# Expert tokens by quarter-row gathers and VectorE block transposes, and three reorderings around the last tile and the choice of tokens

## What is computed

```
x = x + xattn(layernorm(x), ctx)          # attention without softmax over 128 keys
x = x + fp6_ffn(layernorm(x))             # operands quantised in blocks of 32, dequantised, multiplied
x = x + mix(layernorm(x), ctx)            # x @ W1.T + a mean of ctx @ W2.T + b
x = x + moe(layernorm(x))

logits = x @ Wg + bg;  probs = softmax(logits over the tokens)      # 16 experts
vals, idx = top_k(probs per batch and expert, 128)
tok = x[idx]                                                        # 128 tokens of 512
h = relu(tok @ w1 + b1); h = relu(h @ w2 + b2); h = h @ w3 + b3     # per expert, 512x512 each
out[idx] += h * vals
```

## Time and profile before

| | |
|---|---|
| median of 3 runs | 740.56 us (740.15 to 741.81) |
| the profiled execution | 738.98 us |
| its span in the trace | 737.2 us |
| busy, share of the span | PE 97%, DVE 71%, ACT 55%, POOL 57% |
| DMA | 118 MB, mean 160 GB/s |
| mean granted TensorE clock | 0.99 of full |

### The profile page before, as it was taken

How to read it: one execution, slowest core, us unless ns; L and a number is a source line. 1 busy time by engine, 2 the same in 40 slices (tenths; PEclk the granted TensorE clock), 3 DMA queues, 4 the chain that set the end, 5 groups by cost and what they waited for, 6 DMA issues and landing times.

```text
span 737.2 us, 12752 instructions
## 1 busy us (share of the span) xinstructions
PE 714.1 (97%) x4506; PEld 623.2 (85%) x4506; DVE 520.4 (71%) x978; ACT 402.0 (55%) x680; POOL 421.6 (57%) x621
## 2 busy tenths in 40 slices
PE   6999999999999999999999899999999999999995
PEld 5765888888888888888888878798999899899894
DVE  5785789889888898875897798463664556363561
ACT  5755444454554445868668533454664556464641
POOL 2825789888888887876878722604430442340132
PEclk9999999999999999999999999999999999999998
DMA  8710122222212213110116998796895798995544
GB/s 311 267 30 15 44 73 76 76 85 73 89 60 87 86 58 103 44 61 29 61 60 242 334 401 296 191 366 186 234 372 165 192 355 268 298 274 157 143 86 58
DMA packets 61671, 118.04 MB, mean 160 GB/s; under 512 B 6056, under 2 KB 7464, under 8 KB 61608
## 3 DMA queue, kind: packets, MB, share of 16 engines
q1 hardware_dynamic: 54312, 100.44, 38.9%
q0 software_dynamic: 7296, 16.78, 10.3%
HBM read 91.76 MB, written 25.21 MB: 159 GB/s over the span
## 4 chain that ended last, share of the span: by engine, by line
PE 84%; issue 5%; DMA 3%; DVE 3%; POOL 2%; ACT 2%; POOLq 0%; DVEq 0%; ACTq 0%
PE bank L356 39%; PE banks L356 9%; PE bank L363 6%; PE bank L1004 6%; PE banks L871 4%; PE banks L877 3%; DMA out<-y,ids 3%; PE banks L1004 2%; PE banks L881 2%; PE banks L882 2%; PE banks L1431 1%; PE bank L1326 1%; PE banks L1035 1%; PE bank L1048 1%; DMA tok<-xn,ids 0%
## 5 line engine op out<-in xcount | busy, mean ns | idle before, releaser
L2851 POOL DMA_INDIRECT out<-y,ids x24 | 46.1, 1923 | 156.8 <-DVE y L2562 155.0
L1982 DVE TENSOR_TENSOR w_l<-w_raw,w_h 128x2048 fp32r<-128x2048 f32 x35 | 80.1, 2290 | 62.8 <-ACT w_h L1505 58.5
L1970 DVE BATCH_NORM_STATS2 bn<-x 128x6 f32<-128x512 f32 x112 | 77.0, 687 | 8.0 <-DMA x<-x 5.2
L1505 ACT ACTIVATE w_h<-w_raw 128x2048 fp32r<-128x2048 f32 x36 | 68.5, 1918 | 7.1 <-DMA w_raw<-w 7.1
L1901 ACT ACTIVATE h<-bank,b 128x512 f32<-128x512 f32 x48 | 33.1, 689 | 63.0 <-PE bank L356 60.0
L1982 DVE TENSOR_TENSOR hT_l<-h,hT_h 128x512 fp32r<-128x512 f32 x48 | 33.0, 690 | 40.3 <-ACT hT_h L1907 38.1
L356 PE MATMUL bank<-tokT_h,w_h 128*128 128x256 f32 x188 | 55.1, 293 | 0.0
L356 PE MATMUL bank<-tokT_h,w_l 128*128 128x256 f32 x188 | 53.2, 283 | 0.0
L356 PE MATMUL bank<-tokT_l,w_h 128*128 128x256 f32 x188 | 53.2, 283 | 0.0
L2614 POOL TENSOR_SCALAR rstd<-mean_var 128x1 f32<-128x1 f32 x108 | 25.9, 239 | 47.2 <-DVE mean_var L1975 42.2
L356 PE MATMUL bank<-wf_h,xdT_h 128*128 128x512 f32 x128 | 52.7, 412 | 0.0
(11 more groups left out here) (426 smaller groups left out, 2377.3 us busy)
## 6 DMA issues: line engine op xcount, KB each, us to landing
w_raw<-w SPq DMA_DIRECT2D x36, 1024.0 KB
early_w<-w SPq DMA_DIRECT2D x24, 1024.0 KB, 10.6
x<-x SPq DMA_DIRECT2D x32, 256.0 KB, 2.8
xn<-xn SPq DMA_DIRECT2D x32, 256.0 KB
out<-x SPq DMA_DIRECT2D x29, 256.0 KB, 2.5
mask<-mask_t SPq DMA_DIRECT2D x8, 256.0 KB, 3.3
slot_all<-slots SPq DMA_DIRECT2D x4, 512.0 KB, 7.8
stage<-wk SPq DMA_DIRECT2D x1, 1024.0 KB, 7.8
```

Source lines behind the costliest of these rows:

```text
L1505: act.activation(dst, src, ACT.Copy).then_inc(sem, 1)
L1970: dve.bn_stats(bn6[which][:, j % 2, :], src[:, :]).then_inc(sem_bn[which], 1)
L1982: dve.tensor_tensor(dst, src, hi_part, ALU.subtract).then_inc(sem, 1)
L2851: pool.indirect_dma_start(out=out_rows, out_offset=bass.IndirectOffsetOnAxis(ap=ids[:, r:r + 1], axis=0), in_=y[e % 2][b][:, :], in_offset ...
```

## The change

Stage 2, experts 2 to 11: PE's eight transposes per expert go. POOL fetches each batch's tokens by four gathers of quarter rows (512 bytes for each of 128 partitions), so that partition 32q+k gets quarter q of token 32t+k. DVE turns 32x32 blocks (`turn_tokens`), reading its input with a step of four elements, into `tok_raw`, which lies where `tok_l` lies and is written once `hidden(e, 0)` has read `tok_l`. ACT makes the high part in one 128x1024 instruction, DVE the low part in place. Feature 4p+c is now on partition p of chunk c, so layer 0 weights are loaded with four neighbouring rows (8 KB) per partition, and the PE transposes that stay (experts 0 and 1, early experts, singles) read their input with a step of four elements. Quarter ids are made once: ACT repeats the ids, PE makes four small transposes, DVE adds the quarter's number. In POOL's turn after a single's expert the single's gather and add and the first add come ahead of the eight gathers.

Choice: `from_neighbour` is interleaved with `early_outputs(2)`, half of `early_outputs(3)` no longer stands ahead of the transpose of the ids, ACT's exponential comes before `early_weighted(2)`, POOL's third early add behind the gathers. Last tile: POOL's mix bias and third rstd of tile 31 come one turn earlier, ahead of a gather; ACT's `find(0)` goes behind the logit rows, `early_copy(0)` and `norm4(29)` change places. Turn 27: four shifted additions go from DVE to POOL. SP issues an early weight load ahead of two stores.

```diff
+    def of_chunk(rows, c):
+        return rows[:, c::C]
+    def turn_blocks(eng, out, rows):
+        return eng.transpose(out.rearrange("p c (t k) -> p t c k", k=QBLK),
+                             rows.rearrange("p (t k c) -> p t c k", t=P // QBLK, c=C))
+    def expert_weights(layer, e):
+        w = io.w[layer][e]
+        return w.rearrange("(p c) n -> p c n", c=C) if layer == 0 else chunked(w)
...
-        early_outputs(2)
-        pe.wait_ge(sm.a_w, 1)
-        warm, spare = w_h[0], ps_hid[3]
+        early_outputs(2, 0, 2)
+        spare = ps_hid[2]
         pe.wait_ge(sm.k_half, 1)
         from_neighbour(other_v, lv[LAST_LISTS][:, :])
+        early_outputs(2, 2, 3)
         pe.wait_ge(sm.k_half, 2)
         from_neighbour(other_i, li[LAST_LISTS][:, :])
-        early_outputs(3, 0, 2)
+        early_outputs(2, 3, C)
         pe.wait_ge(sm.k_ids, 1)
         pe.transpose(ps[1][:, 0:HEADS], top_i[:, :], ident[0:HEADS, 0:HEADS]).then_inc(sm.k_tr, 1)
-        keep_warm(3, warm, spare)
+        early_outputs(3, 0, 1)
         pe.wait_ge(sm.k_out, 1)
         pe.transpose(ps[0][:, 0:HEADS], top_v[:, :], ident[0:HEADS, 0:HEADS]).then_inc(sm.k_tr, 1)
-        early_outputs(3, 2, C)
+        early_outputs(3, 1, C)
...
         pe.wait_ge(sm.k_pos, 2)
-        keep_warm(9, wh, spare)
+        pe.wait_ge(sm.a_rep, 1)
+        for t in range(C):
+            last = pe.transpose(ps[5][:, 2 * t * ROWS:2 * t * ROWS + HEADS], exps[0:HEADS, t * P:(t + 1) * P],
+                                ident[0:HEADS, 0:HEADS])
+        last.then_inc(sm.k_tq, 1)
+        keep_warm(7, wh, spare)
...
-            if e + 1 < JOINT:
+            if e + 1 < TURNED:
                 tokens(e + 1)
...
+        def turned_hi(e):
+            act.wait_ge(sm.d_tr, B * (e - 1))
+            hi(sm.a_thi, tok_h[:, :, :], tok_raw[:, :, :])
...
+        def turn_tokens(e):
+            dve.wait_ge(sm.p_h, 4 * e - 2)
+            for b in range(B):
+                dve.wait_ge(sem_tok[e % 2][b], tokens_in(e))
+                turn_blocks(dve, tok_raw[:, :, b * P:(b + 1) * P], tok[e % 2][:, b, :]).then_inc(sm.d_tr, 1)
+        def turned_lo(e):
+            dve.wait_ge(sm.a_thi, e + 4)
+            lo(sm.d_tlo, tok_l[:, :, :], tok_raw[:, :, :], tok_h[:, :, :])
...
             hidden_lo(e, 0, 1)
-            if e + 1 < JOINT:
+            if e + 1 < TURNED:
                 token_lo(e + 1)
+            elif e + 1 < JOINT:
+                turn_tokens(e + 1)
             for n in range(2):
                 if nxt < len(order):
                     split_lo(nxt)
                     nxt += 1
                 if e >= 1:
                     weighted(e - 1, n)
+                if n == 0 and TURNED <= e + 1 < JOINT:
+                    turned_lo(e + 1)
...
+                if k == N:
+                    mix_bias(N - 1)
+                    rstd_of(2, N - 1, sm.d_st3, sm.g_r3)
                 if k in (N - 1, N):
                     gather_early(k - N + 1)
...
+                if k == 27:
+                    places_in_column()
...
+        def gather_quarters(e):
+            if e < 2 * TURNED:
+                pool.wait_ge(sm.p_tok, B * (e - 1))
+            else:
+                pool.wait_ge(sm.d_tr, B * (e - 3))
             for b in range(B):
                 r = b * E + FIRST + e
+                for t in range(C):
+                    pool.indirect_dma_start(
+                        out=tok[e % 2][:, b, t * P:(t + 1) * P], out_offset=None, in_=xn4_quarters,
+                        in_offset=bass.IndirectOffsetOnAxis(ap=quarter_ids[:, t, r:r + 1], axis=0),
+                    ).then_inc(sem_tok[e % 2][b], 16)
...
         for e in range(JOINT):
+            if e - 1 in SINGLE:
+                if SINGLE[e - 1] + 1 < FIRST:
+                    gather_single(SINGLE[e - 1] + 1)
+                add_single(SINGLE[e - 1], e - 1)
+                add(e - 1, 0)
             if e + 2 < JOINT:
-                gather(e + 2)
+                gather_quarters(e + 2)
```

More of the change, by code:

```diff
@@ L119, in build @@
     segbase = place("segbase", [P, 1])
+    quarter = place("quarter", [P, 1])
     bq = place("bq", [P, C])
@@ L364, in four_transposes, with four_row_transposes @@
         return last
+    def of_chunk(rows, c):
+        return rows[:, c::C]
+    def four_row_transposes(pe, bank, rows):
+        for c in range(C):
+            last = pe.transpose(bank[:, c * P:(c + 1) * P], of_chunk(rows, c), ident[:, :])
+        return last
+    def turn_blocks(eng, out, rows):
[4 more added lines that the diff above has]
+        return w.rearrange("(p c) n -> p c n", c=C) if layer == 0 else chunked(w)
     def blocks(t):
@@ L702, in load_raw @@
                 lo_done(sp, i - RAW)
-            sp.dma_start(w_raw[i % RAW][:, :, :], chunked(io.w[layer][FIRST + e])).then_inc(sem_raw[i % RAW], 16)
+            sp.dma_start(w_raw[i % RAW][:, :, :], expert_weights(layer, FIRST + e)).then_inc(sem_raw[i % RAW], 16)
         def load_single(s, layer):
@@ L963, in placed @@
             pe.wait_ge(sm.e_dve, CV["marked"])
+            pe.wait_ge(sm.e_pool, CG["places"])
             pe.wait_ge(sm.c_cut, 48)
@@ L1755, in _ @@
                     sums4(j)
-            if k >= 29 and SUMMED.start <= k - 4 < N - 1 and not fourth_later(k - 4):
+            if k == N + 1:
+                early_copy(0)
+            if k == N + 2:
+                norm4(N - 3)
+            if k >= 29 and k != N + 1 and SUMMED.start <= k - 4 < N - 1 and not fourth_later(k - 4):
                 norm4(k - 4)
@@ L1791, in _ @@
                 slots_in_rows()
-            if k == 31:
-                find(0)
             if k == 0:
@@ L1820, in _ @@
                     .then_inc(sm.a_seg, 1)
+            if k == 31:
+                find(0)
         def early_relu(e, layer):
@@ L1929, in _ @@
         token_hi(0)
+        split_hi(2)
         nxt = AHEAD
@@ L2252, in tiles @@
                 return marks[0][:, i * FIRST:(i + 1) * FIRST, 8:].rearrange("p e (s a) -> p e s a", a=GRP)
-            then(dve.tensor_tensor(tiles(0), logits, limit(0), ALU.is_gt))
-            then(dve.tensor_tensor(tiles(1), logits, limit(1), ALU.is_ge))
-            end = 8 + N // B
-            for src, dst, shift in ((0, 1, 1), (1, 2, 2), (2, 1, 4)):
-                then(dve.tensor_tensor(marks[dst][:, :, 8:end], marks[src][:, :, 8:end],
-                                       marks[src][:, :, 8 - shift:end - shift], ALU.add))
-            dve.tensor_tensor(marks[2][:, :, 8:end], marks[1][:, :, 8:end], marks[1][:, :, 0:end - 8], ALU.add)                .then_inc(sm.e_dve, 1)
+            dve.tensor_tensor(tiles(0), logits, limit(0), ALU.is_gt)
+            dve.tensor_tensor(tiles(1), logits, limit(1), ALU.is_ge).then_inc(sm.e_dve, 1)
         def token_slots():
@@ L2534, in _ @@
         dve.wait_ge(sm.k_pos, 2)
+        dve.wait_ge(sm.k_tq, 1)
+        dve.tensor_scalar(quarter_ids[:, :, :],
+                          ps[5][:, 0:2 * C * ROWS].rearrange("p (t r) -> p t r", t=C)[:, :, 0:HEADS:2],
+                          quarter[:, 0:1], None, ALU.add).then_inc(sm.k_quart, 1)
         def split_lo(i):
@@ L2708, in gather_early, with places_in_column @@
             ).then_inc(sem_tok_e[e], 16)
+        def places_in_column():
+            pool.wait_ge(sm.e_dve, CV["marked"])
+            end = 8 + N // B
+            for src, dst, shift in ((0, 1, 1), (1, 2, 2), (2, 1, 4)):
+                then(pool.tensor_tensor(marks[dst][:, :, 8:end], marks[src][:, :, 8:end],
+                                        marks[src][:, :, 8 - shift:end - shift], ALU.add))
+            pool.tensor_tensor(marks[2][:, :, 8:end], marks[1][:, :, 8:end], marks[1][:, :, 0:end - 8], ALU.add)\
+                .then_inc(sm.e_pool, 1)
         for k in range(LAST + 1):
@@ L2932 @@
     arrays["later"] = -(p[:, None] > p[None, :]).astype(np.float32)
+    arrays["quarter"] = (p // 32).astype(np.float32).reshape(P, 1)
     arrays["segbase"] = (p // 64 * 2048 + p % 4 * 512).astype(np.float32).reshape(P, 1)
```

88 lines of the change are left out of this document (49 added, 39 removed).

## The result

The changed kernel takes 746.2 us (median; 737.5 to 750.1) where the kernel before, run beside it on the same chip, takes 740.1: a ratio of 1.0069, with a 95% interval of 1.0056 to 1.0081. It is slower by 5 to 6 us; 730.8 was forecast. The medians are 6.2 us apart; the ratio, which leaves out two runs of a slower state of the chip (748.9 and 750.1 us), says 5.1. The profiled execution took 745.9 us with a span of 744.1, so 6.9 us more than the one of before (737.2).

The account below looks back on a forecast made before the run. Stage 2 was taken as bound by TensorE (PE). The terms, -8.7 + 2.0 - 0.9 - 1.1 - 1.1 = -9.8 us, taken from a median of 740.56, gave 730.8 us; range 725 to 739.

Parts of the forecast that it names:

- Term 1: Stage 2, experts 2 to 11: PE loses eight transposes each, all on the path, -8.7 us; a plain expert becomes 17.0 us.
- Term 2: New token path on DVE and ACT in stage 2: turns of 0.69 us each, hidden behind PE with 3.4 us slack.
- Term 3: GpSimd's queue in stage 2: eight gathers take about 12.4 us; PE stalls 1.0 us after experts 1 and 4; +2.0 us.
- T: The end of hidden(e, 0) in stage 2, from which the prediction counted the times of the new token path.
- late gathers cost PE more: Rival, stage 2: PE stalls 3 us at three places, 9 us in place of 2, giving 737.8 us; chance 0.15.
- Terms 4 and 5: Turn 27, four additions moved to POOL: -0.9 us; last tile, rstd a turn earlier: -1.1 us.
- Term 6: The choice: ids' transpose about 1.7 us earlier, +0.6 us of PE work before tokens(0); sum -1.1 us.
- GpSimd's lock: Stage 2: an indirect DMA starting within DVE's subtraction of two SBUF tensors waits for it; eight gathers 12.4 rather than 10.6 us.
- The rival in which GpSimd becomes the bound: Stage 2: gathers averaging about 1.6 us or more make GpSimd decide; 753 us at 2.0 us a gather; chance 0.10.
- Step of four on PE: PE's 48 remaining transposes read with a step of four: taken as zero cost, bound above +5.3 us.
- the rival at half speed: PE's remaining transposes read a step of four at half speed: 736.1 us; chance 0.13.
- Weights: Rival, stage 2: the saved time returns as PE's wait for weights, 737.5 us; chance 0.05.

Follow-up runs that it names:

- gathers_first: The changed kernel with expert e+2's eight gathers ahead of both adds in GpSimd's turn after a single's expert: 731.0 us, ratio 0.9876 to the kernel before.
- filled_before_weights: The changed kernel with 24 filler matmuls of constants ahead of hidden(4, 0) and hidden(7, 0), before PE waits for anything: 741.3 us, ratio 1.0014 to the kernel before.
- free_ids: The changed kernel with GpSimd's 4.5 us subtraction for the first expert's w_l made to wait for DVE's token_ids: 743.5 us, ratio 1.0042 to the kernel before.
- y_before_low: The changed kernel with DVE's weighted(e - 1, 1) ahead of the second split_lo in the turn after a single: 744.1 us, ratio 1.0055 to the kernel before.

## Why the prediction was wrong

The range ended at 739 and *slower* had 0.11. By its own steps:

- **Term 1 (-8.7) was right.** A plain expert takes 16.99 us (517.47 to 534.46), 0.85 less. Without the waits, stage 2 is 10.0 us shorter.
- **Term 2 had one size wrong and held.** The turn takes 1.10 us, not 0.69; the earlier trace rows have a step of two, and I carried "a step costs nothing" from PE to DVE. (Those rows do not even show it for two: a column costs 1.0 ns there, and 0.8 with a step of one.) It lies inside the bound of 1.38, and the slack hid it where the gathers are in time: gathers_first has the same turns and no wait.
- **Term 3 is the step that failed.** "The add ends near T + 9.1 behind turned_lo" overlooked that split_lo follows turned_lo at once; it ended at T + 11.7. Of these 2.6 us 2.2 are the subtraction, and 0.3 are turned_lo, late by the longer turns. "It lands 2.6 us after its issue ends" came from the first gather of stage 2; with the DMA engines busy in full (share 1.06 from 540 to 545 us) it was 4.6 (that the load is the cause is argued, not tested). The eight gathers, with the gap before each, took 12.0 us instead of my 12.4. Together 2.6 + 2.0 - 0.4 = 4.2, so the stall of 1.0 should be 5.2, and it was 5.0 (5.8 at the second place). The order of events, the two places and the silence at the third (its add too took 4.48 us) were as predicted; where nothing is left to hide behind, each error ahead goes to PE whole. The rival *late gathers cost PE more* had this mechanism and 3 us for it.
- **What no term had: the clock.** 2 x 5.75 us of matmuls took 16.1. A stall of PE was priced as its length; filled_before_weights shows that not quite half as much comes on top (4.6 on 10.8 us).
- **Terms 4 and 5 were right in their rows and half wrong in their sum.** POOL's additions took 369.25 to 371.13, as counted, and PE's wait became 0.8 us shorter; in the last tile the idle time of POOL before the last rstd is gone. But together they stood for 2.0 us, and `seg_logits` came 0.96 us earlier. What was gained by turn 28 was gone by turn 32. There POOL, ready at 399.25, waits 0.81 us for the slots of find(0), which ACT now works out behind the logit rows, and starts at 400.06. It had started at 400.08 without a wait, and its next rstd stands at 405.06 in both kernels. The prediction had put this move at nothing, "since POOL is the limit". The cost named beside the terms, early_tokens(1) behind its gather, was not covered either: it held PE 2.09 us, so that the first product of an early expert starts at 417.48 instead of 415.91, and PE is the bound of the choice.
- **Term 6 (-1.1) was wrong in its premise.** It counted what DVE and the ids gain. Even with the 3 us lock taken out (free_ids), the chain is PE's from 416 us on, as it was before, and the same PE work in another order is nearly as long: from the second block of 64 products of the early experts (423.49) to hidden(0, 0) it takes 45.96 us, and it took 46.15. What the ids' instruction could meet was in the trace of before, as two rows of POOL and DVE that overlap only for the last 0.24 us of the first:

```profile
439.93 4.54 POOL L2632 TENSOR_TENSOR w_l<-w_raw,w_h 128x2048 fp32r<-128x2048 f32 x1 [1.31 <-ACT w_h L1505]
...
444.23 0.31 DVE L2384 TENSOR_SCALAR pack<-pos,segbase 128x104 f32<-128x104 uint32 x1
```

  The change starts the first 1.8 us later and the second 1.0 us earlier, so that the second falls into the middle of the first, and no term asked about that.
- **GpSimd's lock** was in the right direction: the Trainium skill, page "SBUF — State Buffer", section "Who interferes with whom", infers that descriptor generation is free of DVE's tensor_tensor; y_before_low's 2.29 for 4.49 us speaks against it. (The ids that an indirect DMA takes lie in SBUF too. Whether the reading of them is held or the making of the descriptors, no run here separates.) The rival in which GpSimd becomes the bound wanted 1.6 us a gather; it is 1.31 on average, and turns without a single wait for nothing. **Step of four on PE**: 0.1 us for eight, the rival at half speed falls. **Weights**: PE waits for none in gathers_first.

gathers_first measures 731.0 us where 730.8 was forecast, but partly by chance: in its profile stage 2 starts 2.4 us later, where 3.1 us of gain were counted, there is no stall, where 2.0 were counted, and 1.5 us come from behind the last add, where nothing was.

## What to carry to other kernels

When a queue feeds a saturated engine, put what the engine will wait for ahead of what nobody waits for, and do it before costing anything: the same instructions in another order were 731 instead of 746 us. If a slack comes out near zero, price the stall with every late bound in front of it and add the clock's fall behind it. Before a reordering is credited with a gain, read whose chain the stretch is: moving work inside one engine's own unbroken chain saves nothing.

## What the runs showed of the hardware

- After a wait of 5 to 5.8 us in which PE did nothing, the next 48 matmuls took 8.60 and 7.50 instead of 5.75 us, at granted clocks of 0.53 and 0.50. With fillers in the wait they took 5.76, at 1.00.
- An indirect DMA on GpSimd that starts while DVE subtracts two tensors in SBUF ends at a nearly fixed distance behind the subtraction: the adds 1.4 to 1.5 us, nearly all gathers 0.8 to 0.9 us. An add takes 1.54 to 1.63 us alone, 3.36 beside one subtraction of 2.28, 4.49 beside two that follow without a gap, 2.29 beside a short one; a gather takes 0.94 to 1.02 alone and up to 2.88 beside one. A copy of one tensor did the same (adds of 2.23 to 2.55 us), a block transpose did not (1.60 and 1.61).
- The other way round, GpSimd's 4.52 us subtraction held a 0.27 us tensor_scalar of DVE for 3.09 us (2.89 to 3.94 in other profiles), until it ended, while DVE's searches in the same rounds were not slower.
- DVE's 128x512 transpose took 0.70 us with a step of one element and 1.10 with a step of four; PE's transposes went from 0.11 to 0.12 us.
